# Gated cross-attention block with a router: statistics by bn_stats in the loop, Newton roots and scaling on GpSimd, router stages one step earlier

## The chip, the cores and the metric

The kernel runs on one core of one Trainium2 chip. The metric is the device time of that core in microseconds (us). Before the change the median of 3 runs is 1148.31 us (1146.42 to 1148.62).

## What is computed

32 sequences of 56 rows and 128 channels attend, with 16 heads of depth 8, to a context of 1500 rows each; then a mixture of 160 experts follows, of which a router takes the top 8 per row. Cut to what matters here:

```
x = x + tanh(g_xattn) * attention(layernorm(x), ctx)          # 32 x 56 rows, context 32 x 1500
y = layernorm(x)                                             # the statistics that the change touches
probs = sigmoid(y @ router_w.T + expert_bias)                # 160 experts
top_w, top_idx = top_k(probs, 8);  top_w = 2.5 * top_w / sum(top_w)
combine = scatter(top_w at top_idx)                          # rows x 160
x = x + tanh(g_ffn) * (sum_e combine_e * down_e(silu(gate_e(y))) + shared(y))
```

## The kernel before

**Attention.** The 32 batches go through a software pipeline of 35 steps (0 to 34), each cut into 12 places k = 0 to 11; the function `body` of each engine is one step. In step s TensorE makes the keys of batch s (line 1177), the row maxima's products (21 per batch, line 1153) and the values (1189) of batch s-1, the scores (1134) of batch s-2 from k = 3 on and of s-3 up to k = 2, their products with the values (1120), and the sums and the output projection (1201, 1213) of batch s-3. ScalarE (ACT in the rows) takes the exponentials (670) and evacuates banks; VectorE (DVE) takes the 21 maxima (879) from a ring of three PSUM banks, the reciprocal of the sums (980), the normalised output (984) and, every second step, the new residual rows of a pair of batches into `xt` (963). GpSimd (POOL) splits the context and the experts' weights into fp16 parts (479 to 517) and spreads queries over head masks: `q_blk` (556) and `q_st` (572). SyncE (SP) issues most transfers. Each engine follows the order in which its code is written.

**Order around the change.** A table gives places `(step, k)` to extra stages, and `aside` (265) runs one when its engine comes to that place. B is 32, so (B, 0) is the start of step 32. In steps 32 to 34 no new keys are made, and in 33 and 34 there are no maxima. The 16 pairs of batches are split into EARLY (pairs 0 to 11) and LATE (12 to 15). For EARLY the second layer norm runs in step 32: `centre` (801), ACT's `square` (585), `variance` (808), ACT's `root` with a load of the square root's table (594), `scale` (814). Then `tokens` transposes four pairs at a time (PE 1223), copies them to `q_hi` (ACT 690), `xnT` and `q_lo` (DVE 918, 919); `logits` (1235) multiplies them by the router's weights in four groups of three pairs; `biased` (921) adds the bias into `prob`; `sigmoid` (692); `largest` (933) takes the top 8 and masks them; `router_weights` (944) makes `comb`; `weights_out` transposes it (1253) and copies it to `combT` (ACT 696), which SP stores and reads back spread over partitions (425, 418). LATE does the same behind the last step. `prob` lies over the key parts, `combT` over `q_stk`, `comb` over the context's buffer; the waits of `biased`, `weights_out` and `largest` guard these.

```
CENTRE_AT, VAR_AT, SCALE_AT = (B, 0), (B, 2), (B, 3)
TOKENS_AT = {(B, 5): 0, (B, 9): 1, (B + 1, 0): 2}
LOGITS_AT = {(B + 1, 1): (0, 1), (B + 1, 2): (2, 3)}
PROB_AT, TOP_AT, COMB_AT = (B + 1, 3), (B + 1, 4), (B + 1, 8)
COMBT_AT = {(B + 1, 11): 0, (B + 2, 0): 1, (B + 2, 1): 2}
```

**Experts.** Behind the tail of LATE a loop takes 80 pairs of experts: PE up (1285) and down (1313), ACT silu and high part (760, 766), DVE the weighing and low part (1016, 1022).

Of the kernel before, what the change touches and what calls it, by code (L numbers as in the profile page):

```python
# [14 lines left out]
def flamingo_gated_block(nc, x, ctx, g_xattn, g_ffn, Wq, bq, Wk, bk, Wv, bv, Wo, bo,  # L15
# [3 lines left out]
    ALU = mybir.AluOpType  # L19
# [63 lines left out]
    with stk:  # L83
# [34 lines left out]
        stat = sb("stat", [PT, 5, NP])  # L118
        xnT = sb("xnT", [D, N])
# [34 lines left out]
        def flat(ap, pattern, dt=None):  # L154
# [38 lines left out]
        LGB = [bank[2], bank[3], bank[7], bank[5], bank[3], bank[0]]  # L193
# [3 lines left out]
            ln_sub ln_sq ln_var ln_root rstd_made table_loaded ln_done xn_tr xn_cp bqs_made gates_made bv_made  # L197
# [8 lines left out]
         ln_sub, ln_sq, ln_var, ln_root, rstd_made, table_loaded, ln_done, xn_tr, xn_cp, bqs_made, gates_made, bv_made,  # L206
# [18 lines left out]
        IDENT, MASKS, K_ONES, V_ONES = 2, 11, 12, 14  # L225
        NSMALL = 4
# [12 lines left out]
        def num(hu):  # L239
            return hu[0] * 2 + hu[1]  # L240
# [208 lines left out]
        def _(pool):  # L449
# [134 lines left out]
        def _(act):  # L584
# [4 lines left out]
            def load_root_table(n, sq, some):  # L589

                act.activation(sq[:, 0, 0:1], some, ACT.Sqrt).then_inc(table_loaded, 1)
                act.wait_ge(table_loaded, 1 if n == 1 else 2)
# [41 lines left out]
            load_root_table(1, sq_first, ones_d[0:PT, 0:1])  # L634
# [26 lines left out]
            def body(step):  # L661
                for k in range(KT):
                    j, bt, there = tile_at(step, k, 0)
                    for f in range(2):
# [9 lines left out]
                        if f == 0 and k % TPC == 1 and on(step, 1):  # L674
# [5 lines left out]
                          (VAR_AT, lambda: square(3, sq_early, *EARLY)), (SCALE_AT, lambda: root(3, *EARLY)),  # L680
                          *((at, lambda c=c: tokens(c)) for at, c in TOKENS_AT.items()),
                          (PROB_AT, lambda: sigmoid(1, *EARLY)),
                          *((at, lambda c=c: weights_out(c)) for at, c in COMBT_AT.items()))
# [11 lines left out]

            def weights_out(c):

                if c == 0:
                    act.wait_ge(qst_made, B)
                for a in range(2):  # L700
                    act.wait_ge(cb_tr, 2 * c + a + 1)
                    act.activation(combT[0:EP, a, c * TC:(c + 1) * TC], CTB[2 * c + a][0:EP, 0:TC],
                                   ACT.Copy).then_inc(cb_cp, 1)
# [47 lines left out]
            weights_out(NTC - 1)  # L751
# [35 lines left out]
        def _(dve):  # L787
# [94 lines left out]
            def body(step):  # L882
                for k in range(KT):
# [12 lines left out]
                    if on(step, 1) and k == NEG_AT - 1:  # L896
# [8 lines left out]
                          (CENTRE_AT, lambda: centre(*EARLY)), (VAR_AT, lambda: variance(3, sq_early, *EARLY)),  # L905
                          (SCALE_AT, lambda: scale(3, *EARLY)),
                          *((at, lambda c=c: tokens(c)) for at, c in TOKENS_AT.items()),
                          *((at, lambda g=g: biased(g)) for at, g in LOGITS_AT.items()),
                          (TOP_AT, lambda: largest(1, *EARLY)), (COMB_AT, lambda: router_weights(*EARLY)))
# [23 lines left out]
            def largest(g, p0, p1):  # L933
# [3 lines left out]
                dve.wait_ge(split_lo, B * NCH)  # L937
# [108 lines left out]
        def _(pe):  # L1046
# [176 lines left out]
            def tokens(c):  # L1223

                if c == 0:
                    pe.wait_ge(ln_done, 3)
# [3 lines left out]
                else:  # L1230
                    pe.wait_ge(ln_done, 4)
# [3 lines left out]
            def logits(groups):  # L1235
                for q in groups:
# [16 lines left out]
            def weights_out(c):  # L1253
# [119 lines left out]
```

## Time and profile before

| | us |
|---|---|
| median of 3 runs | 1148.31 (1146.42 to 1148.62) |
| the profiled execution's own time | 1148.09 |
| its span, first to last instruction | 1146.6 |
| PE / DVE / ACT / POOL busy in the span | 1068.3 / 970.7 / 853.4 / 597.1 |
| mean granted TensorE clock | 0.979 of full speed |

The span is what the trace shows; 1.49 us of the execution's time lie outside it. A busy engine isn't for that reason the bound: what counts is which wait ends last in a stretch.

### The profile page before, as it was taken

Reading aid. Unit: us, or ns where it says so; the run is one execution under the profiler, and the core shown is the slowest. Engines: PE = TensorE matmul, PEld = TensorE weight load, DVE = VectorE, ACT = ScalarE, POOL = GpSimd, SP = SyncE. Lnnn points to the kernel's source line nnn. Section 1 sums busy time; section 2 is a strip of 40 time slices with the busy share of each in tenths; the row PEclk is TensorE's granted clock in tenths of the full one; section 3 lists DMA queues with packets and bytes.
Section 4 is the critical chain, followed back from the end, with each engine's and each line's share of the span. In section 5 each row is a group of like instructions: output and inputs, shape, how many; then the busy total and the mean of one; then the engine's idle time right before and its main releaser. Section 6 shows DMA issues by size and latency. Waiting matters only on the chain.

```text
span 1146.6 us, 37955 instructions
## 1 busy us (share of the span) xinstructions
PE 1068.3 (93%) x12090; PEld 707.9 (62%) x12090; DVE 970.7 (85%) x1674; ACT 853.4 (74%) x1825; POOL 597.1 (52%) x1011
## 2 busy tenths in 40 slices
PE   3698899999999999999999997779999999999998
PEld 1366677777677777777777775644555555555554
DVE  4767788888788888888888888658999999999998
ACT  3465677777777777767777776657888888888887
POOL 5797888888888888888888883000000000000000
PEclk9789999999999999999999999979999999999999
DMA  7876867777677687577676642146776777677773
GB/s 154 154 160 159 188 141 189 154 159 169 147 162 174 140 185 161 142 173 157 166 167 139 159 113 60 20 132 189 234 237 224 233 233 228 223 240 231 226 235 118
DMA packets 201815, 197.05 MB, mean 172 GB/s; under 512 B 161999, under 2 KB 168207, under 8 KB 201782
## 3 DMA queue, kind: packets, MB, share of 16 engines
q1 hardware_dynamic: 188292, 174.14, 59.5%
q0 software_dynamic: 11520, 20.99, 6.6%
q10 hardware_dynamic: 1970, 1.49, 0.6%
q8 instruction: 18, 0.29, 0.1%
q14 instruction: 15, 0.12, 0.0%
HBM read 109.96 MB, written 12.55 MB: 107 GB/s over the span
## 4 chain that ended last, share of the span: by engine, by line
PE 52%; DVE 13%; POOL 13%; issue 12%; SPq 5%; DMA 2%; ACT 1%; POOLq 1%; DVEq 0%; ACTq 0%
PE bank L1313 15%; PE bank L1285 15%; PE bank L1120 6%; DVE part_max L879 6%; PE bank L1134 5%; PE bank L1153 5%; DVE rec L980 3%; PE bank L1189 2%; POOL ctx_parts L492 2%; PE bank L1177 2%; POOL q_st L572 2%; POOL q_blk L556 2%; POOL w_in L465 1%; POOL w_in L467 1%; SPq L384 1%
## 5 line engine op out<-in xcount | busy, mean ns | idle before, releaser
L670 ACT ACTIVATE p_exp<-bank 125x448 f32<-125x448 f32 x768 | 400.3, 544 | 195.2 <-PE bank L1134 193.9
L879 DVE TENSOR_REDUCE part_max<-bank 128x1 f32<-128x500 f32 x672 | 420.7, 672 | 78.7 <-PE bank L1153 78.0
L1134 PE MATMUL bank<-q_st,k_stk 97*125 97x224 f16 x1536 | 276.0, 264 | 15.4 <-DMA q_st<-neg_row 8.6
L1153 PE MATMUL bank<-kparts,q_blk 128*128 128x500 f16 x672 | 256.4, 385 | 19.5 <-DVE part_max L879 16.5
L1134 PEld LDWEIGHTS bank<-q_st,k_stk 97*125 97x125 f16 x1536 | 197.2, 139 | 81.0 <-ACT p_exp L670 18.4
L1313 PE MATMUL bank<-ctT,w_ring 128*128 128x448 f16 x960 | 234.0, 353 | 3.0 <-DVE ctT L1022 3.0
L760 ACT ACTIVATE ctT<-bank 128x448 f32<-128x448 f32 x320 | 173.7, 543 | 40.4 <-PE bank L1285 15.9
L1022 DVE TENSOR_TENSOR ctT<-k_stk,ctT 128x448 f16<-128x448 f32 x320 | 198.0, 619 | 0.3 <-ACT ctT L766 0.2
L1120 PE MATMUL bank<-p_exp,v_sb 125*25 125x168 f32 (+1 forms) x6144 | 188.3, 264 | 0.6 <-ACT p_exp L670 0.6
L766 ACT ACTIVATE ctT<-k_stk 128x448 f16<-128x448 f32 x320 | 181.8, 568 | 3.5 <-DVE k_stk L1016 3.4
L1285 PE MATMUL bank<-q_hi,w_ring 128*128 128x448 f16 x640 | 174.1, 354 | 2.4 <-ACT k_stk L748 2.4
L1120 PEld LDWEIGHTS bank<-p_exp,v_sb 125*25 125x25 f32 x6144 | 143.2, 104 | 43.9 <-ACT p_exp L670 1.1
L1016 DVE TENSOR_TENSOR k_stk<-v_sb,ctT 128x448 f32<-128x448 f32 x240 | 149.5, 623 | 9.1 <-DMA v_sb<-c_scratch 3.0
L1313 PEld LDWEIGHTS bank<-ctT,w_ring 128*128 128x128 f16 x960 | 91.5, 97 | 93.3 <-DVE ctT L1022 22.9
L494 POOL TENSOR_TENSOR ctx_parts<-ctx_in,ctx_parts 128x512 f16<-128x512 f32 x96 | 110.9, 1155 | 8.0
L1285 PE MATMUL bank<-q_lo,w_ring 128*128 128x448 f16 x320 | 113.0, 353 | 0.0
L1285 PEld LDWEIGHTS bank<-q_hi,w_ring 128*128 128x128 f16 x640 | 62.5, 98 | 61.8 <-issue 2.6
L971 DVE SCALAR_TENSOR_TENSOR kparts<-bank,bkc,kparts 128x500 f16<-128x500 f32 x93 | 68.1, 732 | 35.7 <-ACT kparts L736 35.7
L1153 PEld LDWEIGHTS bank<-kparts,q_blk 128*128 128x128 f16 x672 | 65.0, 97 | 45.6 <-DVE part_max L879 27.2
L465 POOL DMA_DIRECT2D w_in<-in_L_ffn_w_gate_dram x160 | 85.7, 536 | 5.7
L1189 PE MATMUL bank<-wv_hi,ctT 128*125 128x128 f16 x768 | 84.7, 225 | 0.0
L1189 PEld LDWEIGHTS bank<-wv_hi,ctT 128*125 128x125 f16 x768 | 78.3, 141 | 2.9 <-issue 2.7
(149 smaller groups left out, 1231.6 us busy)
## 6 DMA issues: line engine op xcount, KB each, us to landing
v_sb<-c_scratch SPq DMA_DIRECT2D x114, 448.0 KB, 3.9
k_stk<-kparts SPq DMA_DIRECT2D x384, 93.8 KB
ctx_in<-in_ctx_dram SPq DMA_DIRECT2D x30, 672.0 KB
k_stk<-c_scratch SPq DMA_DIRECT2D x38, 448.0 KB, 3.9
w_scratch<-w_out POOLq DMA_DIRECT2D x80, 128.0 KB, 3.5
w_in<-in_L_ffn_w_gate_dram POOLq DMA_DIRECT2D x160, 32.0 KB, 3.2
w_in<-in_L_ffn_w_down_dram POOLq DMA_DIRECT2D x80, 64.0 KB, 3.5
ctx_in<-in_ctx_dram SPq DMA_DIRECT2D x30, 78.0 KB
```

The source lines that it names most:

```text
L670: act.activation(p_exp[0:KP, j % PR, f * 448:(f + 1) * 448], ST[f][0:KP, 0:448], ACT.Exp).then_inc(exp_done, 1)
L760: act.activation(s_act[:, t % 2, :], ZB[t][:, 0:TC], ACT.Silu).then_inc(s_done, 1)
L766: act.activation(h_hi[:, t, :], h_f[:, t, :], ACT.Copy).then_inc(hh_done, 1)
L879: v.reduce_max(part_max[:, i // NCH, i % NCH:i % NCH + 1], SM[i % NSM][:, 0:CK], axis=AX.X).then_inc(sm_maxed, 1)
L1016: v.tensor_tensor(h_f[:, t, :], c_ring[q][:, t * TC:(t + 1) * TC], s_act[:, t % 2, :], ALU.mult).then_inc(h_done, 1)
L1022: v.tensor_tensor(h_lo[:, t, :], h_f[:, t, :], h_hi[:, t, :], ALU.subtract).then_inc(hl_done, 1)
L1120: last = pe.matmul(OB[32 * (g % 4):32 * (g % 4) + VW, at:at + w], v_sb[0:KP, u, j, g, 0:VW], p_exp[0:KP, j % PR, src:src + w], start=(j == ...
L1134: last = pe.matmul(ST[f][0:KP, (g % 2) * GC:(g % 2 + 1) * GC], k_stk[0:97, u, g, j * KP:(j + 1) * KP], q_st[0:97, u, g, :, :].rearrange("p ...
L1153: pe.matmul(SM[i % NSM][:, 0:CK], rows, kparts[:, u, 0, c * CK:(c + 1) * CK], start=True, stop=True).then_inc(sm_done, 1)
L1189: last = pe.matmul(VB[0:KP, i * D:(i + 1) * D], ctT[:, u, c, part, i, 0:KP], w[:, :], start=(n == 0), stop=(n == 2))
L1285: last = pe.matmul(ZB[t][:, 0:TC], w_ring[:, q, a, :], xparts[b][:, t * TC:(t + 1) * TC], start=(j == 0), stop=(j == 2))
L1313: last = pe.matmul(YB[t][:, 0:TC], w, hparts[b][rows, t, :], start=(shared and i == 0), stop=(end and i == 2), skip_group_check=True)
```

## The change

Statistics of each pair's 128 channels are taken by one `bn_stats` in the loop, a step after the pair's rows are written, and `bn_aggr` turns them into mean and variance in step 30. For EARLY GpSimd makes the inverse roots by four Newton steps on 112x12 tiles and scales pair by pair; ACT's square and root and DVE's four passes go from step 32. Tokens, logits, bias, sigmoid and top 8 move up by some 4 to 9 places. The copies to `combT` move from ACT to DVE. LATE uses the same statistics with ACT's root. VectorE's loop ends two steps sooner (steps 30 and 31 are written out). ACT's table of the square root for LATE is loaded from a constant.

```diff
-    CENTRE_AT, VAR_AT, SCALE_AT = (B, 0), (B, 2), (B, 3)
-    TOKENS_AT = {(B, 5): 0, (B, 9): 1, (B + 1, 0): 2}
-    LOGITS_AT = {(B + 1, 1): (0, 1), (B + 1, 2): (2, 3)}
-    PROB_AT, TOP_AT, COMB_AT = (B + 1, 3), (B + 1, 4), (B + 1, 8)
+    AGGR_AT = (B - 2, 2)
+    TOKENS_AT = {(B, 1): 0, (B, 4): 1, (B, 7): 2}
+    LOGITS_AT = {(B, 9): (0,), (B, 10): (1,), (B, 11): (2,), (B + 1, 0): (3,)}
+    BIASED_AT = {(B, 10): (0,), (B, 11): (1, 2), (B + 1, 0): (3,)}
+    PROB_AT, COMB_AT = (B + 1, 0), (B + 1, 7)
+    TOP_AT = {(B + 1, 1): (0, 6), (B + 1, 3): (6, 12)}
...
-        LGB = [bank[2], bank[3], bank[7], bank[5], bank[3], bank[0]]
+        LGB = [KB, bank[2], bank[3], KB, bank[3], bank[0]]
...
+            def then(ins):
+                steps[0] += 1
+                ins.then_inc(newton, 1)
+                pool.wait_ge(newton, steps[0])
+            def normalise_early(p0, p1):
+                pool.wait_ge(mv_made, p1)
+                var, root, half, t = (nst[:, i, p0:p1] for i in range(4))
+                then(pool.tensor_scalar(var, mv[:, p0:p1, 1], EPS_LN, None, ALU.add))
+                then(pool.tensor_scalar(root.bitcast(mybir.dt.int32), var.bitcast(mybir.dt.int32),
+                                        -0.5, float(0x5f3759df), ALU.mult, ALU.add))
+                then(pool.tensor_scalar(half, var, -0.5, None, ALU.mult))
+                for _ in range(NEWTON):
+                    then(pool.tensor_tensor(t, root, root, ALU.mult))
+                    then(pool.tensor_tensor(t, t, half, ALU.mult))
+                    then(pool.tensor_scalar(t, t, 1.5, None, ALU.add))
+                    then(pool.tensor_tensor(root, root, t, ALU.mult))
+                for p in range(p0, p1):
+                    last = pool.tensor_scalar(xc[:, p, :], xt[:, p, :], mv[:, p, 0:1], nst[:, 1, p:p + 1],
+                                              ALU.subtract, ALU.mult)
+                    if p % PPC == PPC - 1:
+                        last.then_inc(xn_made, 1)
             def body(step):
...
+                if isinstance(step[0], int) and num(step) == B:
+                    normalise_early(*EARLY)
                 for c in range(NCH):
...
@@ ACT @@
-                          (VAR_AT, lambda: square(3, sq_early, *EARLY)), (SCALE_AT, lambda: root(3, *EARLY)),
-                          *((at, lambda c=c: weights_out(c)) for at, c in COMBT_AT.items()))
...
-            load_root_table(4, sq_late, stat[:, 2, 0:1])
-            square(4, sq_late, *LATE)
-            root(4, *LATE)
+            load_root_table(2, nst[:, 0, 0:1], ones_d[0:PT, 0:1])
+            root(3, *LATE)
...
-            weights_out(NTC - 1)
@@ DVE @@
+            def statistics(h):
+                at = bass.ds(h, 1)
+                dve.wait_ge(x2_done, h + 1)
+                v.bn_stats(bst[:, at, :].rearrange("p a c -> p (a c)"), xt[:, at, :].rearrange("p a c -> p (a c)"))\
+                    .then_inc(bn_made, 1)
+            def aggregate(p0, p1):
+                dve.wait_ge(bn_made, p1)
+                for p in range(p0, p1):
+                    v.bn_aggr(mv[:, p, :], bst[:, p, :]).then_inc(mv_made, 1)
...
             def evacuate(step, k):
+                if on(step, 4) and k == 0 and back(step, 4)[1] == 1:
+                    statistics(back(step, 4)[0])
...
-            attention(dve, body, first=1)
-            dve.wait_ge(x2_done, NP)
-            centre(*LATE)
-            variance(4, sq_late, *LATE)
-            scale(4, *LATE)
+            attention(dve, body, B - 2, first=1)
+            statistics(NP - 1)
+            aggregate(*LATE)
+            dve.wait_ge(mv_made, NP)
+            v.tensor_scalar(stat[:, 2, LATE[0]:LATE[1]], mv[:, LATE[0]:LATE[1], 1], EPS_LN, None, ALU.add).then_inc(ln_var, 1)
+            dve.wait_ge(ln_root, 3)
+            link(v.reciprocal(stat[:, 4, LATE[0]:LATE[1]], stat[:, 3, LATE[0]:LATE[1]]))
+            for p in range(*LATE):
+                last = v.tensor_scalar(xc[:, p, :], xt[:, p, :], mv[:, p, 0:1], stat[:, 4, p:p + 1], ALU.subtract, ALU.mult)
+            last.then_inc(ln_done, 1)
...
+            weights_out(NTC - 1)
@@ PE @@
             def tokens(c):
+                if c < 3:
+                    pe.wait_ge(xn_made, c + 1)
                 if c == 0:
-                    pe.wait_ge(ln_done, 3)
                     pe.wait_ge(k_lo_done, B * NCH)
...
                     if q == 0:
-                        pe.wait_ge(sm_maxed, B * (MT * NCH))
+                        pe.wait_ge(xl_cp, 3)
+                    elif q == 1:
+                        pe.wait_ge(sm_maxed, B * (MT * NCH) - 2)
                     elif q == 2:
-                        pe.wait_ge(neg_copied, B)
+                        pe.wait_ge(sm_maxed, B * (MT * NCH) - 1)
                     elif q == 3:
-                        pe.wait_ge(xl_cp, 3)
+                        pe.wait_ge(lg_biased, 1)
```

## Rows read from the trace of the kernel before

**Rows 1.** Page of the profile, chain that ended last, by engine.

```profile
PE 52%; DVE 13%; POOL 13%; issue 12%; SPq 5%; DMA 2%; ACT 1%; POOLq 1%; DVEq 0%; ACTq 0%
```

**Rows 2.** Stretches: length, busy PE, PEld, DVE, ACT, POOL; clock, DMA share, GB/s.

```profile
668.30:689.10 20.80, 20.02 (x311) 14.88 (x309) 17.66 (x29) 15.08 (x34) 19.14 (x40) 1.00 0.35 97
689.10:718.00 28.90, 22.61 (x318) 16.62 (x317) 24.89 (x38) 18.73 (x38) 7.81 (x16) 0.94 0.21 55
718.00:742.30 24.30, 18.16 (x270) 13.76 (x268) 17.76 (x52) 16.65 (x29) 0.00 (x0) 0.93 0.14 23
742.30:749.40 7.10, 6.28 (x100) 5.03 (x100) 0.04 (x1) 6.11 (x13) 0.00 (x0) 1.00 0.34 96
749.40:779.20 29.80, 20.07 (x78) 10.68 (x78) 17.90 (x43) 14.52 (x26) 0.00 (x0) 0.77 0.40 124
779.20:1146.60 367.40, 361.31 (x1912) 184.90 (x1912) 356.89 (x639) 320.62 (x636) 0.00 (x0) 1.00 0.68 221
```

**Rows 3.** Groups in step 32 on VectorE: busy us, mean ns, idle before.

```profile
L879 DVE TENSOR_REDUCE part_max<-bank 128x1 f32<-128x500 f32 x21 | 13.0, 670 | 1.8 <-PE bank L1153 1.8
...
L802 DVE TENSOR_REDUCE stat<-xt 112x12 f32<-112x1536 f32 x1 | 1.7, 1743 | 0.0
...
L803 DVE TENSOR_SCALAR stat<-stat 112x12 f32<-112x12 f32 x1 | 0.2, 174 | 0.0
```

**Rows 4.** VectorE's timeline, steps 31, 33, tail: start, length, instruction, idle before.

```profile
671.56 2.66 DVE L879 TENSOR_REDUCE part_max<-bank 128x1 f32<-128x500 f32 x4 [0.73 <-PE bank L1153]
674.95 0.68 DVE L879 TENSOR_REDUCE part_max<-bank 128x1 f32<-128x500 f32 x1 [0.73 <-PE bank L1153]
...
723.70 0.66 DVE L929 TENSOR_TENSOR kparts<-bank,eb_b 112x480 f32<-112x480 f32 x1 [0.55 <-PE bank L1249]
...
769.31 2.22 DVE L1000 TENSOR_TENSOR ctT<-k_stk,ctT 64x448 f16<-64x448 f32 x4
```

**Rows 5.** GpSimd's timeline, the head masks at the start and steps 31, 32.

```profile
2.01 0.20 POOL L472 TENSOR_SCALAR_AFFINE_SELECT head_mask<-head_mask 128x16 f16<-128x16 f16 x1
2.27 0.20 POOL L474 TENSOR_SCALAR_AFFINE_SELECT head_mask<-head_mask 128x16 f16<-128x16 f16 x1
...
680.71 2.32 POOL L572 TENSOR_TENSOR q_st<-q_stk,stack_mask 96x224 f16<-96x224 f16 x4
...
693.13 3.26 POOL L572 TENSOR_TENSOR q_st<-q_stk,stack_mask 96x224 f16<-96x224 f16 x4 [3.08 <-PE bank L1134]
```

**Rows 6.** Groups of GpSimd by form, whole span.

```profile
L512 POOL TENSOR_TENSOR w_out<-w_in,w_out 128x128 f16<-128x128 f32 x80 | 34.2, 427 | 6.5
L509 POOL CAST w_out<-w_in 128x128 f16<-128x128 f32 x80 | 23.3, 292 | 0.0
```

**Rows 7.** TensorE's timeline, steps 32 and 33 and the tail.

```profile
692.05 0.38 PE L1153 MATMUL bank<-kparts,q_blk 128*128 128x500 f16 x1
...
720.57 1.88 PE L1249 MATMUL bank<-rT,xnT 128*112 128x160 f32 x12
...
730.71 1.07 PE L1134 MATMUL bank<-q_st,k_stk 97*125 97x224 f16 x4 [4.42 <-ACT p_exp L670]
...
742.34 1.00 PE L1265 MATMUL bank<-ident,ctx_in 112*80 112x112 f32 x8 [0.57 <-DVE ctx_in L952]
...
759.56 0.60 PE L1054 MATMUL bank<-ident,xc 112*128 112x112 f32 x4 [1.42 <-DVE xc L817]
```

**Rows 8.** Chain of waits, in order of time: start, length, what.

```profile
686.76 0.64 PE bank L1177 x3
...
725.70 1.28 ACT L694
...
728.83 2.81 DVE top L939 x12
...
755.06 0.70 DVE stat L802
...
771.56 0.55 ACT q_stk L702
```

More of the change, by code:

```diff
@@ L118, in flamingo_gated_block @@
         stat = sb("stat", [PT, 5, NP])
+        bst = sb("bst", [PT, NP, 6])
+        mv = sb("mv", [PT, NP, 2])
+        nst = sb("nst", [PT, 4, EARLY[1]])
         xnT = sb("xnT", [D, N])
@@ L205, in flamingo_gated_block @@
         (consts, weights_in, bias_in, small_in, late_in, x_in, x_rest, wp_tr, wp_cp, wp_lo,
-         ln_sub, ln_sq, ln_var, ln_root, rstd_made, table_loaded, ln_done, xn_tr, xn_cp, bqs_made, gates_made, bv_made,
+         ln_sub, ln_sq, ln_var, ln_root, rstd_made, bn_made, mv_made, newton, xn_made, table_loaded, ln_done, xn_tr, xn_cp, bqs_made, gates_made, bv_made,
          q_mm, q_hi_done, q_lo_done, q_rows, q_rest_rows, k_ones, ob_cleared, wo_rows, cv_mm, constant_made, pre_done, sh_tr, sh_cp, sh_lo, o_cleared,
@@ L225, in flamingo_gated_block @@
         IDENT, MASKS, K_ONES, V_ONES = 2, 11, 12, 14
+        NEWTON = 4
         NSMALL = 4
@@ L549, in _ @@
             pool.wait_ge(q_hi_done, 1)
+            steps = [0]
+            def then(ins):
[19 more added lines that the diff above has]
+                        last.then_inc(xn_made, 1)
             def body(step):
@@ L587, in square, with load_root_table @@
                 act.activation(sq, xc[:, p0:p1, :], ACT.Square).then_inc(ln_sq, 1)
-            def load_root_table(n, sq, some):
-                act.activation(sq[:, 0, 0:1], some, ACT.Sqrt).then_inc(table_loaded, 1)
-                act.wait_ge(table_loaded, 1 if n == 1 else 2)
+            def load_root_table(n, at, some):
+                act.activation(at, some, ACT.Sqrt).then_inc(table_loaded, 1)
+                act.wait_ge(table_loaded, n)
             def root(n, p0, p1):
@@ L679, in body @@
                           (GATES_AT, gates_and_shared),
-                          (VAR_AT, lambda: square(3, sq_early, *EARLY)), (SCALE_AT, lambda: root(3, *EARLY)),
                           *((at, lambda c=c: tokens(c)) for at, c in TOKENS_AT.items()),
-                          (PROB_AT, lambda: sigmoid(1, *EARLY)),
-                          *((at, lambda c=c: weights_out(c)) for at, c in COMBT_AT.items()))
+                          (PROB_AT, lambda: sigmoid(1, *EARLY)))
             def tokens(c):
@@ L694, in sigmoid @@
                 act.activation(prob[:, p0:p1, :], prob[:, p0:p1, :], ACT.Sigmoid).then_inc(prob_done, 1)
[L696 to L703, printed above, removed]
             def values(bt, c):
@@ L904, in body @@
                           (CONSTANT_AT, constant_term),
-                          (CENTRE_AT, lambda: centre(*EARLY)), (VAR_AT, lambda: variance(3, sq_early, *EARLY)),
-                          (SCALE_AT, lambda: scale(3, *EARLY)),
+                          (AGGR_AT, lambda: aggregate(*EARLY)),
                           *((at, lambda c=c: tokens(c)) for at, c in TOKENS_AT.items()),
-                          *((at, lambda g=g: biased(g)) for at, g in LOGITS_AT.items()),
-                          (TOP_AT, lambda: largest(1, *EARLY)), (COMB_AT, lambda: router_weights(*EARLY)))
+                          *((at, lambda g=g: biased(g)) for at, g in BIASED_AT.items()),
+                          *((at, lambda p=p: largest(1, *p)) for at, p in TOP_AT.items()),
+                          (COMB_AT, lambda: router_weights(*EARLY)),
+                          *((at, lambda c=c: weights_out(c)) for at, c in COMBT_AT.items()))
                 evacuate(step, KT - 1)
@@ L919, in tokens, with weights_out @@
                 v.tensor_tensor(q_lo[:, cols], TOKB[c][:, 0:TC], q_hi[:, cols], ALU.subtract).then_inc(xl_cp, 1)
+            def statistics(h):
[7 more added lines that the diff above has]
+                    v.bn_aggr(mv[:, p, :], bst[:, p, :]).then_inc(mv_made, 1)
+            def weights_out(c):
+                if c == 0:
+                    dve.wait_ge(qst_made, B)
+                for a in range(2):
+                    dve.wait_ge(cb_tr, 2 * c + a + 1)
+                    v.tensor_copy(combT[0:EP, a, c * TC:(c + 1) * TC], CTB[2 * c + a][0:EP, 0:TC]).then_inc(cb_cp, 1)
             def biased(groups):
@@ L925, in biased @@
                     if q == 0:
-                        for u in range(2):
-                            dve.wait_ge(kst_here[u], (B // 2) * (16 * 3 * HG))
+                        dve.wait_ge(kst_here[0], (B // 2) * (16 * 3 * HG))
+                    if q == 3:
+                        dve.wait_ge(kst_here[1], (B // 2) * (16 * 3 * HG))
                     dve.wait_ge(lg_mm, q + 1)
@@ L1258, in weights_out @@
                     pe.wait_ge(lg_biased, 4)
+                elif c == 1:
+                    pe.wait_ge(neg_copied, B)
                 elif c == 2:
```

12 lines of the change are left out of this document (5 added, 7 removed).

## The prediction

> **What bounds the kernel now.** I read the chain of waits first: over the whole span it lies on TensorE for about half [rows 1]. That is an average, so the second view is the busy time by stretch [rows 2]. It splits the time from the last ordinary step into steps 31 to 34, the tail and the experts. An ordinary step of attention takes 20.80 us with TensorE busy for 20.02: TensorE sets its pace. Step 32, in which the second layer norm runs, takes 28.90 us although it makes no keys; DVE is busy for 24.89 of it, TensorE for only 22.61, with the clock down to 0.94. Step 33 takes 24.30 us with nobody near full. Step 34 takes 7.10 and the tail up to the experts 29.80. The experts' 367.40 us are TensorE's and DVE's, and the change doesn't enter them. So what can move lies between 668 and 779 us, plus whatever the loop of attention pays for its new instruction.
>
> **Loop, one bn_stats per two steps.** It reads 128 columns from SBUF. DVE's reductions take 670 ns for 500 columns and 1743 for 1536 [rows 3], a slope of 1.04 ns a column, so 128 columns are about 0.3 us (an estimate; ends 0.2 and 0.6, if it needs two passes). It stands at k = 1 of the odd steps, behind the maximum that starts at 671.56. DVE then runs four maxima and waits 0.73 us for TensorE before the next [rows 4]. The bn_stats goes into that gap and the three-bank ring keeps TensorE ahead. Cost 0, with the gap as the cover. Without the cover, 14 times 0.3 is 4.2 us before step 32. The pair's own wait is for an x2_done of DVE itself, long given.
>
> **Step 30, twelve bn_aggr** of six numbers each. Nothing of the kind is in the trace; the nearest is a 12-number instruction of 0.17 us [rows 3], and independent ones overlap, so I take 0.12: 1.4 us, of which 0.7 goes into the same kind of gap: cost 0.7 (ends 0 and 3).
>
> **Step 32.** Four DVE passes go, like the 1.74 us one, with three small ones like the 0.17 [rows 3]: 7.7 us. The two token pairs in it become three and move up (a copy and a subtraction of 448 columns each, by the bias's 0.66 for 480 about 0.6, 1.2 together), and three bias groups of 0.66 come in [rows 4]. DVE: 24.9 - 7.7 + 1.2 + 2.0 = 20.4 us, plus some 0.5 us of waiting for ACT's q_hi at each of three tokens, 21.9. TensorE: an ordinary step of 20.8 less three key products of 0.64 [rows 8] is 18.9; plus three token transposes (four matmuls in 0.60 at the low clock, 0.4 taken) and three groups of logits, 1.88/2 = 0.9 each [rows 7]: 18.9 + 1.2 + 2.7 = 22.8 us. The two are near each other and feed each other through three banks. Before, the step took 28.9 - 24.9 = 4.0 us more than its busier engine; I take 1.7 more than TensorE's 22.8, between the 0.8 of the ordinary step and the 4.0: 24.5 us, a gain of 4.4 (ends 2 and 6). ACT loses its square and two table loads there, which were in DVE's shadow: 0 by themselves.
>
> **GpSimd, ahead of that.** It reaches step 32 when the q_st of 680.71 ends, at 683.0 [rows 5]. The statistics wait for it since step 30. Nineteen small instructions each wait for the one before: the head-mask pair shows 0.26 us from start to start with such a wait [rows 5], so 4.9 us. Then per pair one instruction of 128 columns, between the cast's 0.29 and the two-input subtraction's 0.43 [rows 6]: four pairs in 1.2 to 1.7. The first xn_made comes at 683.0 + 4.9 + 1.5 = 689.4, the third at 692.3. TensorE asks for the first after the maxima product of 692.05 [rows 7], about 692.3: 2.9 us of cover, cost 0. Behind it queue, on GpSimd, the last expert pairs and q_st of batch 31: q_st ended at 696.4 [rows 5] and will end near 703; its scores are asked for at k = 3 of step 33, past 715. SP's reads of the stored weights come after step 32's maxima row, so they aren't late either.
>
> GpSimd's 12 pairs cost 3.5 to 5.1 us where one DVE pass over the same took 1.74 [rows 3, 6]: two to three times dearer. The Trainium skill (GPSIMD Engine Reference, Engine selection) sends elementwise work to VectorE, with GpSimd about twice as slow on two inputs; rows 3 and 6 agree. By that rule the passes should stay on DVE, and the sum would lose 1.7 us of gain in step 32. The row says the same price but another place: GpSimd is busy for 7.81 us of 28.90 there [rows 2], so I let its time count as nothing.
>
> **Step 33.** Now TensorE waits 4.42 us [rows 7] while ACT loads the sigmoid's table at 725.70 (1.28), takes the sigmoid until 728.8, and reloads (1.28) [rows 8]; before that four groups of logits (3.8 us, 1.88 for two [rows 7]) and a token transpose delay the scores. DVE then works from the top 8 at 728.83 [rows 8] until TensorE's first comb transpose, which waits for it until 742.34 [rows 7]: 13.5 us of work. After the change, with T the start of step 33: two exponentials to T+1.4, table to 2.7 (the fourth bias group is in by 2.0), sigmoid to 4.5, reload to 5.8. TensorE then has ten places left. Before it took from 730.71 to about 741.8 for seven [rows 7], 11.1 us with the dropped clock in it; ten are 15.8 by proportion and 15 if the low clock is paid once, so it is at k = 11 at T+21. DVE does its 13.5 us from T+4.5 with a pause of some 2.3 before k = 3, where the second half of the top 8 stands behind the output's copy: T+20.3. Both are done at about T+21, against 24.3 from 718.0 to 742.3: gain 3.3 (ends 1.5 and 4.5). The stall for ACT itself doesn't go, it moves to k = 1.
>
> **Step 34.** ACT gives six copies of combT to DVE, which is idle there (0.04 us busy of 7.10, ACT 6.11, TensorE 6.28 [rows 2]). TensorE's 6.3 is then the floor: gain 0.7 (ends 0 and 1).
>
> **Tail.** The last xt is there at 755.04. Until TensorE's transposes at 759.56 run three DVE passes of 0.69, ACT's square, its root, five small ones: 4.5 us [rows 7, 8]. After: bn_stats 0.3, four bn_aggr 0.5, add, root and reciprocal 0.7, four scalings 0.8: 2.3 to 2.8 us. But TensorE was idle for only 1.42 us before 759.56 [rows 7]: it is busy with the shared expert until 758.1, so 1.4 is the gain. Against it: combT's last copy goes behind DVE's four low parts, which end at 771.53 [rows 4]; two copies end at about 772.65, where ACT's ended at 772.10 [rows 8]. The store, the read back and the first weighed product hang on that: loss 0.5. Net gain 0.9 (ends -0.5 and 1.8).
>
> **Sum:** -0.7 + 4.4 + 0 + 3.3 + 0.7 + 0.9 = 8.6 us off the profiled execution's 1148.09 (span 1146.6 and 1.49 around it). That execution is 0.22 under the median, so against the median I predict 1148.31 - 8.6 = 1139.7.
>
> **Rivals.**
> (a) DVE and TensorE stay entangled in step 32 and DVE's router chain ends after TensorE in step 33. For: both pairs of ends lie within 1 us, and the step lost 4.0 us that way before. Then 2 and 2 instead of 4.4 and 3.3: 4.9 gained, 1143.4. Chance 0.22.
> (b) The loop pays for bn_stats: 4.2 us of the gain go, 1143.9. Against: the gap of 0.73 in row after row of the same step. Chance 0.10.
> (c) Slower: GpSimd's chain is late. TensorE's queue would stand at k = 1 of step 32 with scores and maxima behind it. The wait is 683.0 + 19p + 1.5 - 692.3 = 19p - 7.8 us, with p the price of one dependent instruction. It begins at p = 0.41 and eats the whole 8.6 at p = 0.86; at 1.0 the result is 1150.9. Against: p is 0.26 on 16 columns, and only integer or two-input forms could differ. Chance 0.05.
> (d) Nothing lands: step 33's earlier sigmoid is paid by a stall of the same length with a lower clock, and the tail by the copy; 1147.5. Against: rows 8 show DVE on the path, and it is relieved. Chance 0.07.
> (e) More: no entanglement (6), full gain of step 33 (4.5), tail 1.8: 1148.31 - 12.5 = 1135.8, chance 0.12 within the forecast's side.
> The forecast itself has 0.44.
>
> **How the numbers follow.** The likeliest case gives 1139.7. The range runs from (e) to past (b): 1135.3 to 1144.6, which leaves out (c), (d) and some of the edges. What can be told from no change here is about 0.2%, 2.3 us: (c) is slower, (d) no change, the rest faster: 0.88, 0.07, 0.05.
>
> **What would show it.** Windows of equal work: step 32 at about 24.5 us, step 33 to its first comb transpose at 21 to 21.5, that transpose 7 us sooner; no wait of the first token transposes for GpSimd; the idle gap before the fifth maximum of odd steps smaller by one bn_stats while a pair of steps still takes 41.8 us; four scalings ready before the shared expert's third product ends; the DMA of combT 0.5 us later against its comb transposes. A wait of TensorE on xn_made, or odd steps longer by 0.3, would prove me wrong at the named term.

## The result, and the profile after

The changed kernel takes 1140.58 us (median of 5 runs, 1139.9 to 1141.22) against 1148.47 (1146.42 to 1151.15) of the kernel before, run beside it: ratio 0.9928, 95% interval 0.9916 to 0.994, so 6.9 to 9.6 us less. Predicted were 1139.7 us, range 1135.3 to 1144.6. The profiled execution took 1140.58, its span is 1139.1, against 1146.6.

First the view of stretches (step 31, step 32, step 33 up to the first comb transpose, step 34, tail, experts; columns as in [rows 2]). Steps 31 and 32 are cut here at the first score of a step; [rows 2] has its cuts some 0.3 us later, and at the first scores step 31 took 20.76 us before and step 32 29.01.

```profile
668.96:689.67 20.71, 20.01 (x312) 15.01 (x310) 17.57 (x29) 14.75 (x34) 18.32 (x45) 1.00 0.31 85
689.67:713.65 23.98, 22.96 (x344) 18.53 (x339) 20.15 (x34) 15.30 (x36) 21.47 (x41) 1.00 0.27 72
713.65:737.07 23.42, 17.79 (x250) 12.47 (x247) 15.51 (x49) 16.25 (x28) 0.00 (x0) 0.78 0.12 29
737.07:743.48 6.41, 5.98 (x100) 5.03 (x100) 3.39 (x6) 3.62 (x7) 0.00 (x0) 1.00 0.32 90
743.48:771.70 28.22, 19.18 (x78) 10.40 (x78) 17.81 (x49) 12.86 (x23) 0.00 (x0) 0.82 0.43 135
771.70:1139.10 367.40, 361.29 (x1912) 184.94 (x1912) 356.79 (x639) 320.54 (x636) 0.00 (x0) 1.00 0.69 221
```

Step 32 went from 29.01 to 23.98 us and is TensorE's again: busy 22.96, clock 1.00. Step 33 hardly moved, and its mean granted clock is 0.78; that is the surprise. The experts are untouched. Cut finer, at starts and ends of single instructions in both traces (reciprocal of the sums, first score of a step, first comb transpose, copies, the store, the first down product that waits for the weighing), the spans differ by:

| stretch | before | after | gain | predicted |
|---|---|---|---|---|
| start to the reciprocal in step 29 | 638.64 | 639.58 | -0.9 | 0 |
| from there to step 31 | 29.37 | 29.38 | 0 | -0.7 |
| steps 31 and 32 | 49.77 | 44.69 | 5.1 | 4.4 |
| step 33 to the first comb transpose | 24.56 | 23.42 | 1.1 | 3.3 |
| on to the last output copy | 7.02 | 6.41 | 0.6 | 0.7 |
| tail: to the last `xt` | 5.67 | 5.46 | 0.2 | 0 |
| tail: to its token transposes | 4.53 | 2.65 | 1.9 | 1.4 |
| tail: to the store of `combT` | 12.56 | 13.14 | -0.6 | -0.5 |
| tail: to the first waiting down product | 7.80 | 7.65 | 0.1 | 0 |
| sum, with 0.0 from the experts | | | 7.5 | 8.6 |

The first line isn't the change's. The first such reciprocal, ahead of the first `bn_stats`, is later already (88.73 before, 90.27 after), and in the ten experiments below, whose code is the same up to step 29 but for one, the reciprocal of step 29 starts between 636.20 and 641.45.

That the experts add 0.0 depends on the trace, too. From the first waiting down product to the end the two traces above and three of the experiments take 366.7 to 366.9 us; the seven others take 368.4 to 368.6, and in those the first 5 us behind the same wait ran at a granted clock of 0.66 to 0.68, in the five short ones at 1.00:

```profile
772.38:777.38 5.00, 5.00 (x27) 2.61 (x28) 5.00 (x10) 4.36 (x10) 0.00 (x0) 1.00 0.47 117
```

```profile
767.63:772.63 5.00, 5.00 (x19) 2.19 (x20) 3.61 (x7) 3.03 (x7) 0.00 (x0) 0.68 0.27 73
```

The first is the changed kernel's, the second that of the first experiment below.

VectorE's timeline: the aggregation in step 30, the statistics in step 31, and the tail.

```profile
653.19 0.90 DVE L951 BATCH_NORM_AGGREGATE mv<-bst 112x2 f32<-112x6 f32 x12
...
673.08 0.28 DVE L944 BATCH_NORM_STATS2 bst<-xt 112x6 f32<-112x128 f32 x1
673.28 1.91 DVE L897 TENSOR_REDUCE part_max<-bank 128x1 f32<-128x500 f32 x3
675.92 0.68 DVE L897 TENSOR_REDUCE part_max<-bank 128x1 f32<-128x500 f32 x1 [0.73 <-PE bank L1203]
...
748.97 0.29 DVE L944 BATCH_NORM_STATS2 bst<-xt 112x6 f32<-112x128 f32 x1
749.30 0.38 DVE L951 BATCH_NORM_AGGREGATE mv<-bst 112x2 f32<-112x6 f32 x4
...
750.42 1.11 DVE L1040 TENSOR_SCALAR xc<-xt,mv,stat 112x128 f32<-112x128 f32 x4
```

One `bn_stats` takes 0.28 us, 0.20 from its start to that of the next instruction. The wait of 0.73 ahead of the fifth maximum is as long as in [rows 4]: it was to shrink by one `bn_stats` and didn't, and the pace of the loop didn't change either (333.16 us for eight pairs of steps, 333.19 before). Twelve `bn_aggr` take 0.90 and cost nothing.

GpSimd's timeline in step 32, the first two and the last of the nineteen small instructions, the scalings, `q_st`; then TensorE, where it asks for the first scaled rows, and its one wait for VectorE in the step.

```profile
681.66 2.26 POOL L603 TENSOR_TENSOR q_st<-q_stk,stack_mask 96x224 f16<-96x224 f16 x4
684.01 0.25 POOL L565 TENSOR_SCALAR nst<-mv 112x12 f32<-112x12 f32 x1
684.35 0.21 POOL L566 TENSOR_SCALAR nst<-nst 112x12 int32<-112x12 int32 x1
...
689.45 0.21 POOL L573 TENSOR_TENSOR nst<-nst 112x12 f32<-112x12 f32 x1
689.78 9.34 POOL L575 TENSOR_SCALAR xc<-xt,mv,nst 112x128 f32<-112x128 f32 x12
...
706.42 2.11 POOL L603 TENSOR_TENSOR q_st<-q_stk,stack_mask 96x224 f16<-96x224 f16 x4
```

```profile
693.17 0.55 PE L1104 MATMUL bank<-ident,xc 112*128 112x112 f32 x4
...
705.49 0.39 PE L1203 MATMUL bank<-kparts,q_blk 128*128 128x500 f16 x1 [0.67 <-DVE part_max L897]
...
720.18 1.07 PE L1184 MATMUL bank<-q_st,k_stk 97*125 97x224 f16 x4 [3.67 <-ACT p_exp L701]
...
722.44 1.71 PE L1170 MATMUL bank<-p_exp,v_sb 125*25 125x168 f32 x32
...
726.35 1.71 PE L1170 MATMUL bank<-p_exp,v_sb 125*25 125x168 f32 x32
...
737.07 1.00 PE L1320 MATMUL bank<-ident,ctx_in 112*80 112x112 f32 x8 [0.48 <-DVE ctx_in L994]
```

A scaling takes 0.78 us (9.34 / 12), so the first four are ready at 689.78 + 3.11 = 692.9, and TensorE, in order behind a maxima product of 692.95, asks at 693.17: the cover, the time by which they are early, was 0.3 us. The wait of 4.42 us before scores [rows 7] is now 3.67 and stands at k = 1; behind it the products with the values take 1.71 us instead of 0.97. The clock, in windows of step 33 after, and then before:

```profile
716.50:720.20 3.70, 0.04 (x3) 0.03 (x1) 1.90 (x10) 3.67 (x4) 0.00 (x0) 0.93 0.43 99
720.20:724.80 4.60, 4.31 (x44) 2.88 (x44) 1.89 (x12) 2.36 (x6) 0.00 (x0) 0.50 0.17 38
724.80:729.50 4.70, 4.44 (x44) 3.04 (x43) 2.93 (x18) 2.75 (x6) 0.00 (x0) 0.50 0.00 0
729.50:737.00 7.50, 6.15 (x117) 4.25 (x115) 6.99 (x8) 5.04 (x11) 0.00 (x0) 0.97 0.01 2
```

```profile
730.70:734.70 4.00, 3.97 (x42) 2.83 (x43) 4.00 (x27) 2.16 (x5) 0.00 (x0) 0.57 0.00 2
734.70:742.30 7.60, 6.13 (x118) 4.11 (x116) 7.38 (x11) 5.19 (x11) 0.00 (x0) 1.00 0.01 2
```

Half of full speed is the lower of the clock's two levels, 1.2 GHz. Before, it lasted some 4 us behind the wait, now 9.3, so that step 33's gain was spent there. This is no accident of one execution: the new places without filling take 23.30 to 23.42 us for step 33 in six traces.

### The profile page after: what moved, and what is told of

It reads as the page before. It is cut to its first block, busy times and chain, and to the rows that moved or that the text cites. A ratio compares the mean times of both kernels' runs of the same rounds, so it can differ in the third digit from the quotient of the medians.

```text
span 1139.1 us, 37969 instructions
## 1 busy us (share of the span) xinstructions
PE 1069.6 (94%) x12090; PEld 708.6 (62%) x12090; DVE 969.8 (85%) x1706; ACT 845.1 (74%) x1812; POOL 610.7 (54%) x1042
## 4 chain that ended last, share of the span: by engine, by line
PE 45%; POOL 21%; issue 16%; DVE 9%; SPq 3%; DMA 2%; POOLq 2%; ACT 1%; DVEq 0%; ACTq 0%
PE bank L1368 15%; PE bank L1340 15%; PE bank L1170 4%; PE bank L1184 4%; DVE part_max L897 3%; POOL ctx_parts L495 3%; PE bank L1203 3%; POOL q_st L603 3%; POOL q_blk L585 3%; POOL w_in L468 3%; POOL w_in L470 2%; POOL w_out L516 2%; POOL w_out L515 2%; DVE rec L1024 2%; PE bank L1239 2%
## 5 line engine op out<-in xcount | busy, mean ns | idle before, releaser
L1368 PEld LDWEIGHTS bank<-ctT,w_ring 128*128 128x128 f16 x960 | 91.5, 97 | 93.3 <-DVE ctT L1072 22.8
```

The costliest lines, as they stand in the source:

```text
L1368: last = pe.matmul(YB[t][:, 0:TC], w, hparts[b][rows, t, :], start=(shared and i == 0), stop=(end and i == 2), skip_group_check=True)
```

## The experiments

Each starts from the changed kernel; ratios are to the kernel before on the same chip (medians 1149.49, 1149.79 and 1149.16 in the three batches that were timed), and the changed kernel's own is 0.9928 (0.9916 to 0.994). Most intervals overlap that one, so what a part is worth is read from the stretches of the traces, with the ratio as a check.

**The clock in step 33.** Twenty matmuls keep TensorE busy through ACT's table and sigmoid; they go to a PSUM bank that is free, and nothing reads them.

```diff
+    FILL_AT, FILL = (B + 1, 1), 20
+            def fill():
+                pe.wait_ge(lg_biased, 4)
+                for _ in range(FILL):
+                    pe.matmul(bank[3][:, 0:TC], ident16[:, :], q_hi[:, 0:TC], start=True, stop=True)
```

> The changed kernel with 20 matmuls of 448 columns put into TensorE's 3.67 us wait at k = 1 of step 33 (they write to an idle bank and are read by nobody). Theory: step 33 gained only 1.1 us because TensorE came out of that wait at a granted clock of 0.50 for 9.3 us, and so held back the score products, the sum's product and VectorE's reciprocal behind it. If it stays busy the clock stays near 1.00, two places take 2.7 us again instead of 3.9, and step 33 loses 2 to 2.5 us: about 1138.3. Rival 1, the chain of VectorE (top 8, reciprocal, router weights) sets step 33 by itself: the clock stays up and the time stays within 0.5 us of 1140.6. Rival 2, the clock falls whatever TensorE does there: the low stretch stays, and the 20 matmuls of 0.2 us end at the same time as the wait, 1140.6 or slightly above.

Measured: 1138.18 us, ratio 0.9902 (0.988 to 0.9924). Windows and timeline of the same stretch:

```profile
714.40:718.10 3.70, 3.70 (x21) 1.84 (x21) 1.91 (x10) 3.67 (x4) 0.00 (x0) 1.00 0.55 75
718.10:722.70 4.60, 3.81 (x54) 2.35 (x56) 3.09 (x18) 3.72 (x8) 0.00 (x0) 1.00 0.25 57
722.70:727.40 4.70, 4.18 (x80) 2.94 (x79) 4.44 (x18) 3.26 (x8) 0.00 (x0) 1.00 0.02 3
```

```profile
714.34 3.96 PE L1279 MATMUL bank<-q_hi,ident 128*128 128x448 f16 x20
718.13 0.78 PE L1185 MATMUL bank<-q_st,k_stk 97*125 97x224 f16 x4
...
731.79 1.00 PE L1328 MATMUL bank<-ident,ctx_in 112*80 112x112 f32 x8
```

The clock stays at 1.00, and the first comb transpose comes 20.25 us after the step's start instead of 23.42 (20.24 and 20.25 in the two later versions with this filling). The scores behind it start 6.6 us into the step with the filling and 6.5 without, so it is the clock that differs: the low clock cost 3.2 us, and without it the step takes even less than the 21 predicted. By the ratios this version is 3.0 us faster than the changed kernel, by the medians 2.4. In its profile 2.2 us are lost again between step 34 and the end, 1.65 of them in the experts, whose start has the low clock there. The Trainium skill (TensorE: Matmul & The Clock Gate, What's actually happening) has the slow clock as the default, which activity lifts; the trace agrees, with 9.3 us at 0.50 behind the wait and none with the filling.

**combT's last copy.** Both copies of the last four pairs go back to ACT, behind its high parts.

```diff
@@ ACT, behind the high parts @@
+            for a in range(2):
+                c = NTC - 1
+                act.wait_ge(cb_tr, 2 * c + a + 1)
+                act.activation(combT[0:EP, a, c * TC:(c + 1) * TC], CTB[2 * c + a][0:EP, 0:TC],
+                               ACT.Copy).then_inc(cb_cp, 1)
@@ DVE @@
-            weights_out(NTC - 1)
```

> Undoes one part: the last two copies to combT are made by ScalarE again, behind its four silus and high parts. Theory: in the changed kernel they stand behind VectorE's four low parts, and from the token transposes to the store of combT the tail takes 13.1 us where it took 12.6: that distance falls back by 0.5 to 0.6 us, 1140.0. Rival, the store and its read back are bound by something else in the tail (SyncE's issue, the shared expert): no difference, 1140.6.

Measured: 1139.9 us, 0.9912 (0.989 to 0.9934). From the last sigmoid to the store of `combT` the trace has 7.88 us, against 8.60 in the changed kernel and 8.60 or 8.61 in each of the seven other experiments with the copy on VectorE; the kernel before, with the copy on ACT, had 8.11. So the copy's place costs 0.5 to 0.7 us by the traces; the medians differ by less than they scatter. From the token transposes to the store it is 12.15, against 12.52 to 12.75 in six of those and 13.14 and 13.81 in the changed kernel and in the one with six `bn_stats`: the way to the sigmoid scatters more than the copy costs.

**The move by itself.** The router's stages go back to their old places, with the old banks and waits; statistics and scalings stay as changed.

```diff
-    TOKENS_AT = {(B, 1): 0, (B, 4): 1, (B, 7): 2}
-    LOGITS_AT = {(B, 9): (0,), (B, 10): (1,), (B, 11): (2,), (B + 1, 0): (3,)}
-    PROB_AT, COMB_AT = (B + 1, 0), (B + 1, 7)
-    TOP_AT = {(B + 1, 1): (0, 6), (B + 1, 3): (6, 12)}
+    TOKENS_AT = {(B, 5): 0, (B, 9): 1, (B + 1, 0): 2}
+    LOGITS_AT = {(B + 1, 1): (0, 1), (B + 1, 2): (2, 3)}
+    PROB_AT, COMB_AT = (B + 1, 3), (B + 1, 8)
+    TOP_AT = {(B + 1, 4): (0, 12)}
```

> The changed kernel with tokens, logits, bias, sigmoid, top 8 and router weights at their old places and banks; statistics, Newton roots and scaling on GpSimd and the copies on VectorE stay. Theory: most of the gain is the removal of VectorE's passes from step 32 and the shorter tail. Step 32 loses 7.7 us of VectorE's work and has no third token group, bias or logits, so it comes to 21 to 22 us; step 33 goes back to some 24.6 us. In sum 1138.8 to 1140.0, no worse than the changed kernel. Rival, the earlier places carry a gain of their own of 1.5 us or more: 1142 or above.

Measured: 1141.29 us, 0.9925 (0.9904 to 0.9946). Steps 31 and 32 take 43.62 us, step 33 24.78: together 68.40, against 68.11 with the new places and 74.33 before. So the move alone brought 0.3 us, and of the 6.22 us that steps 31 to 33 gained 5.93 came from the removed passes. The theory had that right by the trace; the median lies between its range and the rival's. The places moved by one to five, not by "some 4 to 9" as the section on the change says: tokens by four or five, logits by two to four, the sigmoid by three, the top 8 by three and one, the router weights by one.

**The move with the clock held.** The same old places, with 23 filling matmuls at (B + 1, 4), where TensorE waits for the sigmoid there.

```diff
+    FILL_AT, FILL = (B + 1, 4), 23
```

> The old places of tokens, logits, sigmoid and top 8 (as in the run with the old places), and 23 filling matmuls in TensorE's wait at k = 4 of step 33. With the old places alone steps 31 and 32 take 43.62 us and step 33 24.78, in sum 68.4; in the changed kernel 44.69 and 23.42, 68.1: the move gained 0.3. Theory: the move is worth about 2.2 us, but the low clock behind its wait hid that. With the wait filled in both, the old places give 43.6 and 23.5 (their low stretch cost only some 1.3 us), 67.1, against 44.69 and 20.25, 64.9. So this run is 2 us above the changed kernel with the filling, about 1140.2. Rival: the places don't matter even with the clock held, and both filled versions are equal, about 1138.2.

Measured: 1142.21 us, 0.9938 (0.9915 to 0.9961): 43.58 and 24.57 us. Filling hardly helps the old places, since there VectorE's router chain ends last:

```profile
734.53 1.00 PE L1326 MATMUL bank<-ident,ctx_in 112*80 112x112 f32 x8 [1.77 <-DVE ctx_in L995]
```

With the clock held, the new places take 44.69 + 20.25 = 64.94 us and the old 68.15: the move is worth 3.2 us, where I expected 2.2, and the low clock took 2.9 of them. The ratios (0.9938 against 0.9902) say 4.1 us, give or take 3.7.

**GpSimd's cover.** Twelve Newton steps instead of four: 32 more dependent instructions, 9.5 us.

```diff
-        NEWTON = 4
+        NEWTON = 12
```

> Eight more Newton iterations on GpSimd, 32 dependent instructions of 0.30 us: its first scaled pairs come 9.5 us later. In the changed kernel they are ready at about 692.9 and asked for at 693.17, a cover of 0.3 us. Theory: nearly all of the 9.5 us is a wait of TensorE at k = 1 of step 32, 8 to 9.5 us: 1148.5 to 1150. Rival, there is slack further on (step 32 is held by VectorE, step 33 by ScalarE's stall) that takes half of it: about 1145.

Measured: 1153.56 us, 1.0028 (1.0012 to 1.0044).

```profile
704.55 1.01 PE L1104 MATMUL bank<-ident,xc 112*128 112x112 f32 x4 [9.24 <-POOL xc L575]
...
708.24 1.71 PE L1170 MATMUL bank<-p_exp,v_sb 125*25 125x168 f32 x32
```

Of 9.5 us added, 9.24 arrive as a wait of TensorE: the cover is 0.3, as the timeline of the changed kernel said. The step grew by 11.88 us (35.86 - 23.98), 2.6 more than the wait: behind it the clock is low again (0.50 from 704.5 to 709.0), which neither theory had in it, and the result lies past both.

**What the scaling's price is made of.** Constants in place of the two per-row operands. The early rows are not normalised in this kernel, so the router's scores aren't the reference's.

```diff
-                    last = pool.tensor_scalar(xc[:, p, :], xt[:, p, :], mv[:, p, 0:1], nst[:, 1, p:p + 1],
+                    last = pool.tensor_scalar(xc[:, p, :], xt[:, p, :], 0.0, 0.75,
```

> The changed kernel with constants in place of the per-row mean and inverse root in GpSimd's twelve scalings (subtract 0, multiply by 0.75), so the early rows are not normalised. In the changed kernel one such instruction of 128 columns takes 0.78 us, where I had expected 0.3 to 0.43. Theory: the per-row operands are what makes it slow, and with constants it takes 0.3 to 0.4 us; the first four pairs are then ready 1.5 us sooner. Rival: the fp32 output or the two operations make it slow, and it stays near 0.78. The time stays as it is in both, since TensorE didn't wait for it: 1140.6.

Measured once: 1138.21 us (1149.72 beside it). That it is 2.4 us under the changed kernel's says nothing of the scaling: its reciprocal of step 29 starts 3.4 us sooner, ahead of every changed instruction, and step 33 takes 23.36 us. GpSimd's groups, first this kernel's, then the changed kernel's:

```profile
L575 POOL TENSOR_SCALAR xc<-xt 112x128 f32<-112x128 f32 x12 | 7.3, 635 | 0.1
```

```profile
L575 POOL TENSOR_SCALAR xc<-xt,mv,nst 112x128 f32<-112x128 f32 x12 | 9.3, 785 | 0.1
```

Per-row operands are 0.15 us of it. The rest stays with constants, so the cast (0.29) and the subtraction into fp16 (0.43) of [rows 6] were no bounds for this form; that it is the float32 output or the two operations in one is only argued.

**VectorE in the loop.** Six `bn_stats` per pair of steps instead of one; five write to a scratch tile.

```diff
+                for e in range(5):
+                    v.bn_stats(bsx[:, at, 6 * e:6 * e + 6].rearrange("p a c -> p (a c)"),
+                               xt[:, at, :].rearrange("p a c -> p (a c)"))
```

> Six bn_stats a pair in the loop where there is one, on the changed kernel; five write to a scratch tile that nobody reads. One takes 0.20 us from start to start, six 1.2 us. Theory: the wait of 0.73 us before the fifth maximum of an odd step covers the first three or so; the rest, 0.5 us, is paid 14 times, about 6 to 7 us: 1147. Rival 1, VectorE is nowhere on the path and pays nothing: 1140.6. Rival 2, there is no cover at all and one more bn_stats costs 0.2 each time: 5 times 0.2 times 14 is 14 us, 1154.6.

Measured: 1143.42 us, 0.9945 (0.9923 to 0.9966), but not in the loop: from the reciprocal near 306 us to that near 640 are 333.94 us, against 333.19 before and 333.16 after. VectorE's timeline in step 31:

```profile
673.42 1.06 DVE L946 BATCH_NORM_STATS2 bsx<-xt 112x6 f32<-112x128 f32 x5
674.39 0.27 DVE L948 BATCH_NORM_STATS2 bst<-xt 112x6 f32<-112x128 f32 x1
674.59 2.42 DVE L898 TENSOR_REDUCE part_max<-bank 128x1 f32<-128x500 f32 x4
676.92 0.73 DVE L1019 SCALAR_TENSOR_TENSOR kparts<-bank,bkc,kparts 128x500 f16<-128x500 f32 x1
```

The five more take 1.0 us, in place of the 0.73 us wait. The trace has 0.8 us more over these eight pairs of steps, 0.1 a pair, where my expectation had each microsecond past the gap paid, so the prediction's cost of 0 for one `bn_stats` holds by far. By the median the kernel is 2.8 us over the changed one, by the ratios 2.0; 14 pairs at 0.1 are 1.4 of it, and in its profile the tail takes 0.7 more (13.81 us from tokens to store against 13.14). The rest isn't explained.

**Scaling on VectorE.** GpSimd keeps the Newton steps; the twelve scalings go to VectorE, four at a time.

```diff
+    SCALE_AT = {(B, 0): 0, (B, 3): 1, (B, 6): 2}
+            def scale_early(c):
+                dve.wait_ge(newton, 3 + 4 * NEWTON)
+                for p in range(c * PPC, c * PPC + PPC):
+                    last = v.tensor_scalar(xc[:, p, :], xt[:, p, :], mv[:, p, 0:1], nst[:, 1, p:p + 1],
+                                           ALU.subtract, ALU.mult)
+                last.then_inc(xn_made, 1)
```

> The changed kernel with the twelve early scalings put back on VectorE, four pairs at a time at (32, 0), (32, 3) and (32, 6); GpSimd keeps the Newton steps. VectorE pays 12 x 0.27 us (the four late scalings took 1.11) = 3.3 us in step 32, where it is busy for 20.15 of 23.98 and TensorE for 22.96. Theory one (the two engines feed each other through three banks, so work on VectorE lengthens the step although its sum would still fit): step 32 goes from 23.98 to 25.2 to 26.8 us and the whole to about 1142 to 1143. Theory two (TensorE alone sets step 32, VectorE's 3.8 us of idle time take the scalings in): 24.0 to 24.5 us and 1140.5 to 1141. Either way GpSimd ends its q_st of the last batch 9 us sooner, with no effect.

Measured: 1144.49 us (1144.13 to 1146.6), 0.9959 (0.9945 to 0.9972). VectorE's and TensorE's timelines, and windows of step 32:

```profile
704.59 1.11 DVE L941 TENSOR_SCALAR xc<-xt,mv,nst 112x128 f32<-112x128 f32 x4
```

```profile
698.07 0.60 PE L1109 MATMUL bank<-ident,xc 112*128 112x112 f32 x4 [1.21 <-DVE xc L941]
...
705.75 0.60 PE L1109 MATMUL bank<-ident,xc 112*128 112x112 f32 x4 [2.09 <-DVE xc L941]
```

```profile
693.00:698.00 5.00, 3.57 (x56) 2.71 (x56) 5.00 (x12) 2.54 (x6) 4.52 (x11) 1.00 0.69 179
...
702.00:706.00 4.00, 1.91 (x39) 1.23 (x38) 3.97 (x9) 0.98 (x2) 0.08 (x1) 1.00 0.09 33
706.00:711.00 5.00, 5.00 (x60) 4.03 (x59) 3.88 (x7) 3.00 (x7) 0.00 (x0) 0.66 0.00 0
```

Steps 31 and 32 take 49.20 us, 4.5 more than in the changed kernel and nearly the 49.77 of before. Theory one had the direction and half the size: VectorE is full from 693 to 706, TensorE waits twice for `xc`, and then the mean clock is 0.66. A scaling costs 0.28 us on VectorE and 0.78 on GpSimd, and yet GpSimd is the better place, against these places in VectorE's order: by 4.5 us in the trace, 3.9 between the medians, 3.6 by the ratios. VectorE doesn't wait for the Newton steps here (they end at 688.1, its first scaling starts at 689.98), but the second and third batch stand right ahead of the transposes that need them. No run has them earlier in VectorE's order, so part of the 4.5 us may be the place and not the engine.

**Both together, and filling in the tail.** Filling in step 33 and the copies on ACT in one kernel:

> Both together: the 20 matmuls in TensorE's wait of step 33, and the last copies to combT on ScalarE. Apart, the first took step 33 up to the first comb transpose from 23.42 to 20.25 us, and the second took the distance from the last sigmoid to the store of combT from 8.60 to 7.88. Theory: they lie one behind the other on the path and add up, 3.9 us off the changed kernel, 1136.7. Rival: what step 33 gives is partly taken back in the tail, where the copies and the low clock stand; 1137.7 or more.

Measured: 1138.13 us, 0.9908 (0.9886 to 0.993). The trace has both parts (20.25 us for step 33, 12.05 from tokens to store), the median is no better than with the filling alone, so that the sum of 1136.7 did not come. With filling at three more waits of step 34 and the tail, the two arguments being the wait (0: the last early copy of `combT`; 6: all biased groups) and the number of matmuls:

```diff
+                          ((B + 2, 7), lambda: fill(0, 11)),
@@ ahead of logits((4, 5)) @@
+            fill(0, 6)
@@ ahead of the first up products @@
+            fill(6, 11)
```

> As the version with filling and ScalarE's copies, with filling matmuls in three more waits of TensorE: 11 before the last output projection, 6 before the last logits, 11 before the first expert's products. Theory: the projection (1.8 to 2.0 us at the low clock) goes to 1.1, the logits, the comb transposes and the first products (1.7 to 0.8) likewise, 1.5 to 2 us off the path: 1.5 to 2 us less than the version without them. Rival: the tail hangs on VectorE, ScalarE and the store of combT, so only the projection's 0.8 us shows; or a filling longer than its wait costs what it gives: within 0.5 us of the version without them.

Measured: 1136.71 us (1132.09 to 1137.89), 0.9883 (0.9859 to 0.9906); tokens to store 11.10 us. It has the lowest median of all, 1.2% under the kernel before, but its interval overlaps those of the two versions with less filling, so that it beats them is not shown.

## Why the prediction was right

The total was 0.9 us off, but through errors that offset one another; that it came so near is partly luck. One term, step 33, was off by a factor of three.

- **Loop and step 30.** Cost 0 for `bn_stats` held, at 0.28 us apiece, and six of them show far more room than the gap of 0.73 that I named as the cover. The gap didn't shrink as I had said it would, so the instruction was taken in somewhere else; where isn't shown. `bn_aggr` cost 0, not 0.7.
- **Step 32**: 5.1 instead of 4.4. TensorE's sum was good (22.8, measured 22.96), VectorE's too (20.4 and 20.15); entanglement cost 1.0 over TensorE instead of 1.7. What I hadn't read is in the trace of before: TensorE waited three times for a maximum and ran its last products at the low clock.

```profile
695.07 0.39 PE L1153 MATMUL bank<-kparts,q_blk 128*128 128x500 f16 x1 [2.03 <-DVE part_max L879]
...
699.39 0.38 PE L1153 MATMUL bank<-kparts,q_blk 128*128 128x500 f16 x1 [1.34 <-DVE part_max L879]
...
709.26 0.38 PE L1153 MATMUL bank<-kparts,q_blk 128*128 128x500 f16 x1 [1.90 <-DVE part_max L879]
...
711.05 1.71 PE L1120 MATMUL bank<-p_exp,v_sb 125*25 125x168 f32 x32
```

  Rival (a) fell for the changed kernel, but scaling on VectorE brings it about.
- **GpSimd.** Cost 0 was right by 0.3 us, where I had counted on a cover of 2.9. The dependent instruction was near (0.30, not 0.26: 5.77 us from 684.01 to 689.78, 0.9 more than I had), the scaling was not: 0.78 against 0.29 to 0.43, 1.6 us more for the first four, because I bounded it by a cast and a form with an fp16 output. Rival (c)'s mechanism is real, as twelve Newton steps show, and it had the wrong variable: the scaling's price took more of the cover than p. The Trainium skill (GPSIMD Engine Reference, Engine selection) sends elementwise work to VectorE. That would have lost 1.7 us by my working; followed in the run, at those places, it lost 3.9, so here the measurement decides against it. The Trainium skill (GPSIMD Engine Reference, Engine selection) calls one-input instructions on GpSimd "roughly line-rate"; this one, with a mean and a root per row beside its input, takes 2.8 times VectorE's time.
- **Step 33**: the step that failed, 1.1 instead of 3.3. I let ten places take "15 if the low clock is paid once", by the length it had before. The mechanism that I had priced was the wait; the low clock after it lasted 9.3 us, not 4. With the clock held the step takes 20.25, so the rest of the working stands. Why the 0.50 lasts longer here stays open: with the old places it lasted 6 us behind the same wait of 4.42 us, against some 4 in the kernel before, so the length of the wait doesn't set it. That a thinner mix of scores and products keeps it low is only argued. The first comb transpose came 5.3 us sooner, not the 7 that I had named as a sign.
- **Step 34**: 0.6 (0.7), TensorE busy for 5.98 of 6.41.
- **Tail**: 1.9 - 0.6 (1.4 - 0.5). The statistics to four scalings take 2.6 us (748.97 to 751.53), as worked out. The cap of 1.4, TensorE busy with the shared expert, was lower here: the last shared products ran at the higher clock, and TensorE waited 0.30 us for `xc`. In four of the experiments the stretch takes 3.04 or 3.05 us instead of 2.65, a gain of 1.5. Of the 0.6, 0.5 lie behind the sigmoid, as predicted for the copy. From the last output copy to the last `xt` profiles of one code differ by up to 0.9 us (4.75 and 5.66), so these terms are known to no better than that.
- **Rival (e)**: its terms add up to 12.3 us and not to the 12.5 that I subtracted (1136.0); nothing hangs on it.

## What to carry to other kernels

When work is moved off an engine that is full, ask where it stands in the order and not only what it costs: the same scaling at 2.8 times the price was worth some 4 us on an engine that stayed just ahead of its reader, against one place in the full engine's order. A wait of TensorE has two prices, its length and the low clock behind it; where a stall can't be removed, matmuls into a free bank that nobody reads can take the second one away. Bound the price of an instruction on GpSimd by one of the same form, operands and output type, and write beside each cover how much of it is left.

## What the runs showed of the hardware

- `bn_stats` on 128 float32 columns takes 0.28 us, one every 0.20 in a row; `bn_aggr` of six numbers about 0.07 each in a row of twelve.
- GpSimd's `tensor_scalar` with two operations on 112x128 float32: 0.78 us with per-row operands, 0.61 with constants (7.3 / 12), against 0.28 on VectorE. Dependent instructions on 112x12 follow each other every 0.30 us.
- Behind one wait of 3.67 us TensorE ran for 9.3 us at a granted 0.50, and 1.71 us for what takes 0.97; with the wait filled, never below 1.00 in that step. After a wait of 9.24 us the same products took 1.71 as well. The experts take 1.7 us more when their first 5 us have a granted clock of 0.66 to 0.68 instead of 1.00.
- Six `bn_stats` where one stood took VectorE 1.0 us more per pair of steps, and the loop's pace changed by 0.1 us in 41.6.
